# First attention by fours of heads: scores two pairs at a time, shifts and exps over two banks, value sums in twos

## The chip, the cores and the metric

The kernel runs on one core of one Trainium2 chip. Its time is the device time in microseconds (us) of one execution, and the median over several is given. A core has five engines, each with an in-order queue of its own: TensorE (PE) multiplies matrices into PSUM, VectorE (DVE), ScalarE (ACT) and GpSimd (POOL) work on SBUF, the first two on PSUM as well, and SyncE (SP) issues transfers. They are held together by semaphores: an instruction waits until a count is reached, and whatever stands behind it in its engine's queue waits with it.

## What is computed

Two layers over x of 4 x 2048 tokens of 256 values, each `x = x + attention(norm(x)) * silu(ffn(norm(x)))`. Only the attention of the first layer is changed. It has 16 heads of 16 values; a segment has 512 tokens, every eighth of which is a key (64 keys):

```python
q, k, v = (qkv[0] * scale, qkv[1], qkv[2])
q4 = q.reshape(B, H, S, SEG, hd)
k4 = k.reshape(B, H, S, SEG, hd)[:, :, :, ::DIL]
v4 = v.reshape(B, H, S, SEG, hd)[:, :, :, ::DIL]
scores = jnp.einsum('bhspd,bhskd->bhspk', q4, k4)
scores = scores.reshape(B, H, S, nb, BLOCK_M, Kn)
c = jnp.max(scores, axis=4, keepdims=True)   # over the 64 queries of a block, for each key
w = jnp.exp(scores - c)
den = jnp.sum(w, axis=-1) + 1e-10
num = jnp.einsum('bhsnmk,bhskd->bhsnmd', w, v4)
out = num / den[..., None]
```

The first layer's ffn is one product with a float8 weight and a bias. The second layer has attention with rotary positions over 2048 tokens and a mixture of eight experts.

## The kernel before

Four phases follow each other: `layers_phase` (the whole first layer, and the second layer's norm, projections and router logits), `attend_phase`, `experts_phase` and `combine_phase`. The change is in `layers_phase` alone. It walks over 16 segments m of 512 tokens; the second layer's projections belong to segment n = m - 1, so that two layers are in work at once. The order on each engine is written out by hand: PE's loop at L533, ACT's at L664, DVE's at L923.

Within a segment the heads go by pairs p = 0 to 7. Keys lie block-diagonally in `kbd`, so one product gives the scores of two heads: 128 partitions (2 heads x 64 keys) by 512 queries, which fills one PSUM bank. For a pair:

- `scores` (PE, L431): one product into the bank of the pair; pairs take the two banks of `sc` and the two of `tb` in turn, and a bank is free when the shift of the pair before last but one is done (L439)
- `shift` (DVE, L814): a maximum over each block of 64 queries (`keymax`, L819) and its subtraction (`shifted`, L821)
- the exp (ACT, L669) into one of NW = 3 buffers `wexp`
- `values` (PE, L443): the product with `vbd`, 64 columns wide, into one half of the single bank `ob`. It gives sums and denominators of two heads. Every even pair waits until the pair of halves before it has been copied (L449)
- `out_copy` (ACT, L585) copies `ob` into `oT` for every four heads; `turn` (PE, L453) turns it into `kv`, and `normalise` (DVE, L825) divides

PE's queue in a segment is: scores 0, 1, 2, values 0, scores 3, values 1, scores 4, values 2, turn 0, scores 5, values 3, scores 6, values 4, turn 1, scores 7, values 5, values 6, turn 2, values 7, `turn_second` (the normalised tokens of the second layer, for segment n, turned through `tb`), then `gate` 0 (L461, the first half of the ffn's product, into `pb`), turn 3, gate 1, and the projections of both layers, which end with the queries of segment m + 1.

On ACT each exp is followed, from pair 3 on every second time, by an `out_copy`; `part0` (L608, a cast of the rotated queries and keys of an older segment, 2048 wide) comes after the last exp, `second_turned` (L591, copies what `turn_second` wrote) after the last `out_copy`. On DVE the shifts stand with, between them, the second layer's normalised tokens (`second_norm`, L906, after shift 0), the end of the float8 rounding (`quantise_rest`, L796, after shift 1), `normalise` and the statistics of the next segment's tokens (`normed_tokens`, L896, after shift 5). POOL rotates halves of older queries and keys and computes inverse square roots (`inverse_root`, L309). SP stores and loads.

## Time and profile before

| what | us |
|---|---|
| median of 3 runs (lowest, highest) | 3757.64 (3751.62, 3771.84) |
| profiled execution, device time | 3755.5 |
| its span, first to last instruction | 3753.7 |
| PE busy | 3214.3 (86%) |
| DVE busy | 2698.2 (72%) |
| ACT busy | 2002.4 (53%) |
| POOL busy | 624.1 (17%) |

The profile is of one execution. "Busy" counts the time in which an engine works on at least one instruction; records of matmuls overlap, since they are pipelined. A product of 32-bit operands shows as two records. In the rows by stage (from:to in us of the span) the stages are: from segment 1's first gate product to segment 15's; from segment 0's first score product to its first gate product; the same for segment 8; from there to segment 9's first score product; and 5 us within segment 8. PEld is the load of PE's weights, the clock is the share of full speed granted to PE. In a row of the order of time, several records of the same kind stand together with their count; the bracket behind it is the time that the engine stood still ahead of it, and what ended that.

### The profile page before, as it was taken

To read this page: it belongs to the slowest core of one execution; us is meant where nothing else is said; L and a number is where in the kernel's file an instruction comes from. 1 tells how busy PE (TensorE), PEld (TensorE's weight loads), DVE (VectorE), ACT (ScalarE), POOL (GpSimd) and SP (SyncE) were. 2 spreads that over 40 slices of the span, in tenths; PEclk is the share of its full clock that TensorE was granted. 3 is DMA by queue.
4 is the path that set the end of the run, shared out by engine and by line. 5 is a ranking of instruction groups with operands and counts; after the bars stand their busy time and mean duration, and the time that the engine had idled before them with its cause. 6 is when DMAs were issued, how large, how long until landed. Compare 5 with 4: busy or idle time off the path is not lost. (4 is left out here: it accounts for less than half of the span.)

```text
span 3753.7 us, 67859 instructions
## 1 busy us (share of the span) xinstructions
PE 3214.3 (86%) x22678; PEld 1759.2 (47%) x22679; DVE 2698.2 (72%) x5118; ACT 2002.4 (53%) x3363; POOL 624.1 (17%) x954
## 2 busy tenths in 40 slices
PE   5888888884688988999899899999879899999976
PEld 3444444442233333333333333333358788888865
DVE  5677777775888877888888888888635556565557
ACT  2333433332177777888778788878842223232224
POOL 1122222221222221000000000000023233223310
PEclk9999999997599998999999999999989999999989
DMA  2122222223312222022222211220032111211149
GB/s 71 56 63 74 79 62 66 71 73 89 53 36 47 47 45 46 11 41 47 47 45 47 47 31 26 40 46 18 18 110 67 59 62 40 81 35 44 46 143 327
DMA packets 252770, 230.55 MB, mean 61 GB/s; under 512 B 60924, under 2 KB 235132, under 8 KB 252156
## 3 DMA queue, kind: packets, MB, share of 16 engines
q1 hardware_dynamic: 236040, 192.39, 20.1%
q0 software_dynamic: 16384, 33.64, 2.8%
q8 instruction: 205, 3.36, 0.4%
q14 instruction: 141, 1.16, 0.1%
HBM read 124.28 MB, written 101.06 MB: 60 GB/s over the span
## 5 line engine op out<-in xcount | busy, mean ns | idle before, releaser
L1488 ACT ACTIVATE at_ex<-at_so,keep_exp_scale 128x512 f32<-128x512 f32 (+1 forms) x2304 | 1348.8, 673 | 442.7 <-PE at_so L1382 239.1
L1515 DVE TENSOR_REDUCE at_best<-at_p 128x1 f32<-128x512 f32 (+3 forms) x2560 | 1393.2, 603 | 254.9 <-PE at_p L1364 164.6
L1364 PE MATMUL at_p<-at_ks,at_qs 48*128 48x512 f16 (+3 forms) x2560 | 805.5, 367 | 166.8 <-DVE at_best L1515 122.4
L1382 PE MATMUL at_so<-at_qs,at_ks 50*128 50x512 f16 (+3 forms) x2560 | 688.5, 358 | 19.0 <-issue 9.9
L1436 PE MATMUL at_ob<-at_ex,at_vs 128*32 128x512 f32 (+3 forms) x5120 | 605.4, 565 | 0.3 <-issue 0.2
L1786 ACT ACTIVATE e_hh<-e_hb,e_b1now 128x512 fp32r<-128x512 f32 x256 | 174.6, 689 | 591.6 <-PE e_hb L1721 514.8
L1364 PEld LDWEIGHTS at_p<-at_ks,at_qs 48*128 48x128 f16 x2560 | 216.6, 94 | 461.4 <-DVE at_best L1515 391.7
L1671 POOL DMA_INDIRECT e_xg<-s_xn,e_token x128 | 142.6, 1114 | 1682.7 <-DVE e_token L1816 1518.3
L1382 PEld LDWEIGHTS at_so<-at_qs,at_ks 50*128 50x128 f16 x2560 | 199.3, 95 | 459.6 <-ACT at_ex L1488 341.6
L1751 PE MATMUL e_ob<-e_w2h,e_hh 128*128 128x256 f32 x1024 | 296.0, 289 | 18.1 <-DVE e_og L1854 15.1
L1752 PE MATMUL e_ob<-e_w2l,e_hh 128*128 128x256 f32 x1024 | 291.8, 285 | 0.0
L1753 PE MATMUL e_ob<-e_w2h,e_hl 128*128 128x256 f32 x1024 | 291.6, 285 | 0.0
L1837 DVE TENSOR_SCALAR e_h<-e_hb,e_b1now 128x512 f32<-128x512 f32 x256 | 191.0, 746 | 116.3 <-ACT e_hh L1786 95.2
L451 PE MATMUL a_ob<-a_wexp,a_vbd 128*64 128x512 f32 x256 | 151.2, 675 | 116.2 <-ACT a_oT L589 91.2
L1719 PE MATMUL e_hb<-e_xh,e_w1h 128*128 128x512 f32 x512 | 210.4, 411 | 43.0 <-DVE e_h L1837 25.4
L1854 DVE TENSOR_TENSOR e_og<-e_ob,e_b2now 128x256 f32<-128x256 f32 x128 | 53.6, 423 | 239.2 <-PE e_ob L1753 202.9
L669 ACT ACTIVATE a_wexp<-a_shifted 128x512 f32<-128x512 f32 x128 | 80.6, 630 | 258.4 <-DVE a_shifted L821 258.4
L1721 PE MATMUL e_hb<-e_xh,e_w1l 128*128 128x512 f32 x512 | 206.8, 404 | 4.3 <-issue 4.3
L1347 PE MATMUL at_p<-at_identb,at_key_mask 64*128 64x64 bf16 x2048 | 208.9, 194 | 0.0
L1751 PEld LDWEIGHTS e_ob<-e_w2h,e_hh 128*128 128x128 f32 x1024 | 198.3, 194 | 21.3 <-DVE e_og L1854 16.5
L1720 PE MATMUL e_hb<-e_xl,e_w1h 128*128 128x512 f32 x512 | 207.5, 405 | 0.0
L1752 PEld LDWEIGHTS e_ob<-e_w2l,e_hh 128*128 128x128 f32 x1024 | 198.7, 194 | 0.0
(213 smaller groups left out, 4548.2 us busy)
## 6 DMA issues: line engine op xcount, KB each, us to landing
s_v<-a_v SPq DMA_DIRECT2D x64, 256.0 KB, 3.0
s_qk<-a_part SPq DMA_DIRECT2D x128, 128.0 KB, 2.4
at_vs<-s_v SPq DMA_DIRECT2D x32, 512.0 KB
s_eo<-at_empty SPq DMA_DIRECT2D x16, 1024.0 KB
e_w<-w SPq DMA_DIRECT2D x16, 1024.0 KB
f_rows<-s_eo SPq DMA_DIRECT2D x32, 512.0 KB, 8.3
at_qs<-s_qk SPq DMA_DIRECT2D x96, 128.0 KB
at_ks<-s_qk SPq DMA_DIRECT2D x96, 128.0 KB
```

The costliest lines, as they stand in the source:

```text
L1347: return pe.matmul(out[:, half * HALF:(half + 1) * HALF], mask[rows, half, :], identb[rows, rows], start=False, stop=last)
L1364: last = pe.matmul(out, qs[rows, buf, p, qt * P:(qt + 1) * P], ks[rows, buf, p, ch * SEG:ch * SEG + w], start=True, stop=ch != qc)
L1382: last = pe.matmul(so[:, v % NST, at:at + w], ks[rows, r, p, kt * P:(kt + 1) * P], qs[rows, r, p, q0:q0 + w], start=True, stop=not diag)
L1436: last = pe.matmul(ob[h * HW:(h + 1) * HW, SEG - w:SEG], vs[:, r, kt, h * HW:(h + 1) * HW], ex[:, (G * s + h) % NE, at:at + w], start=(kt ...
L1488: ev.done(act.activation(ex[:, v % NE, 0:width], so[:, v % NST, 0:width], ACT.Exp, scale=keep["exp_scale"][:, 0:1]), "ex")
L1515: ev.done(dve.tensor_reduce(best[:, row:row + 1, ch], p1[:, (at + e) % NP1, 0:wide(item)], AX, ALU.max), "mx")
L1719: pe.matmul(out, ah, bh, start=(j == 0), stop=False)
L1720: pe.matmul(out, ah, bl, start=False, stop=False)
L1721: last = pe.matmul(out, al, bh, start=False, stop=(j == len(pairs) - 1))
L1751: pe.matmul(out, high, w2h[:, u, m, :], start=(m == 0), stop=False)
L1752: pe.matmul(out, high, w2l[:, u, m, :], start=False, stop=False)
L1753: last = pe.matmul(out, low, w2h[:, u, m, :], start=False, stop=(m == HC - 1))
```

## The change

Heads go by fours ("doubles", d = 0 to 3, two pairs each). Both pairs' scores are written one behind the other into two adjacent banks, `sc` for even d and `pb` for odd ones (`tb` is no longer used for scores). Maxima, subtraction and exp each cover both banks in one instruction. Both pairs' value products go out one behind the other, into the two halves of `ob`. The order on PE becomes: scores 0, 1, 2, values 0, `turn_second`, scores 3, values 1, turn 0, values 2, turn 1, values 3, turn 2, gate 0, turn 3, gate 1. On ACT every exp from the second on is followed by the copy of the double before; `second_turned` goes behind the second exp's copy and `part0` ahead of the last copy. On DVE the order is shift 0, the second layer's tokens, shift 1, the rest of the rounding, shift 2, normalise 0, shift 3, normalise 1, the next segment's statistics, normalise 2. `gate` waits for the fourth shift, since `pb` holds scores until then.

```diff
@@ -148,7 +148,6 @@
         bqk1 = sb("bqk1", [P, 4])
         wvg1 = sb("wvg1", [P, DC, D + E])
         bv1 = sb("bv1", [P, D])
-        NW = 3
         x = sb("x", [P, 2, TT, D])
         stats = sb("stats", [P, 2, TT, 6])
         mv = sb("mv", [P, 2, TT, 2])
@@ -167,9 +166,9 @@
         qT = sb("qT", [P, DC, SEG])
         kbd = sb("kbd", [P, DC, H // DC, KN])
         vbd = sb("vbd", [P, H // 2, 2 * HW])
-        keymax = sb("keymax", [P, 2, NBLK])
-        shifted = sb("shifted", [P, 2, SEG])
-        wexp = sb("wexp", [P, NW, SEG])
+        keymax = sb("keymax", [P, 2, 2 * NBLK])
+        shifted = sb("shifted", [P, 2, 2, SEG])
+        wexp = sb("wexp", [P, 2, 2, SEG])
         oT = sb("oT", [P, 2, SEG])
         den = sb("den", [P, TT, G])
         rden = sb("rden", [P, TT, G])
@@ -205,13 +204,13 @@
         ob = ps("ob", [P, SEG])
 
 
-        def bank(p):
-            return sc[:, p % 4, :] if p % 4 < 2 else tb[:, p % 4 - 2, :]
-
-        NP0 = H // 2
+        def banks(d):
+            return sc if d % 2 == 0 else pb
+
+        NP0, ND0 = H // 2, H // 4
         counts = dict(
             var=1, rstd=1, xn=1, tr=1, trc=2, q=2, qc=2, kv=1, kvc=1, ff=2, ffc=2, quant=1, clip=1, round=2, wide=3,
-            s=NP0, shift=NP0, wexp=NP0, pv=NP0, oc=4, ot=4, norm=4, ytr=1, ytc=2,
+            s=NP0, shift=ND0, wexp=ND0, pv=NP0, oc=4, ot=4, norm=4, ytr=1, ytc=2,
             so=2, sog=2, ez=2, gate=1, x1=1, x1_out=1,
             var1=1, rstd1=1, xn1=1, xn1_out=1, tr1=1, tr1c=2, pj=4, pjc=4, rot=1, rot1=1, p1=1, p2=1,
             qk_out=4 * PART, vj=4, vjc=4, lc=4, v_out=NG, l_out=1)
@@ -428,27 +427,32 @@
                                          start=(k == 0), stop=(k == DC - 1))
                     ev.done(last, "q")
 
-                def scores(m, p):
-
-                    if p == 0:
+                def scores(m, d):
+
+                    f = d // (ND0 // DC)
+                    if d == 0:
                         ev.wait(pe, "kvc", m, 1)
                         ev.wait(pe, "sog", m, 0)
-                    f, a = p // (NP0 // DC), 2 * (p % (NP0 // DC))
-                    if a == 0:
-                        ev.wait(pe, "qc", m, f + 1)
-                    ev.wait(pe, "shift", m, max(p - 3, 0))
-                    ev.done(pe.matmul(bank(p), kbd[:, f, a:a + 2, :].rearrange("p a k -> p (a k)"),
-                                      qT[:, f, :], start=True, stop=True), "s")
-
-                def values(m, p):
-                    ev.wait(pe, "wexp", m, p + 1)
-                    if p == 0 and m >= 2:
+                        ev.wait(pe, "qc", m, 1)
+                    if d == 1:
+                        ev.wait(pe, "qc", m, 2)
+                    if d >= 2:
+                        ev.wait(pe, "shift", m, d - 1)
+                    for i in range(2):
+                        a = 2 * ((2 * d + i) % (NP0 // DC))
+                        ev.done(pe.matmul(banks(d)[:, i, :], kbd[:, f, a:a + 2, :].rearrange("p a k -> p (a k)"),
+                                          qT[:, f, :], start=True, stop=True), "s")
+
+                def values(m, d):
+                    ev.wait(pe, "wexp", m, d + 1)
+                    if d == 0 and m >= 2:
                         ev.wait(pe, "vjc", m - 2, TT)
                         ev.wait(pe, "lc", m - 2, TT)
-                    if p % 2 == 0:
-                        ev.wait(pe, "oc", m, p // 2)
-                    r = (p % 2) * 2 * HW
-                    ev.done(pe.matmul(ob[r:r + 2 * HW, :], vbd[:, p, :], wexp[:, p % NW, :], start=True, stop=True), "pv")
+                    ev.wait(pe, "oc", m, d)
+                    for i in range(2):
+                        r = i * 2 * HW
+                        ev.done(pe.matmul(ob[r:r + 2 * HW, :], vbd[:, 2 * d + i, :], wexp[:, d % 2, i, :],
+                                          start=True, stop=True), "pv")
 
                 def turn(m, g):
 
@@ -461,7 +465,7 @@
                 def gate(m, f):
 
                     ev.wait(pe, "quant", m, 1)
-                    ev.wait(pe, "qc", m, f + 1)
+                    ev.wait(pe, "shift", m, ND0)
                     for t in (2 * f, 2 * f + 1):
                         i = 0
                         for w in wf_piece:
@@ -532,17 +536,18 @@
                     queries(0, f)
                 for m in range(NSEG):
                     n, more = m - 1, m + 1 < NSEG
-                    for p in range(NP0):
-                        scores(m, p)
-                        if p >= 2:
-                            values(m, p - 2)
-                        if p >= 4 and p % 2 == 0:
-                            turn(m, (p - 4) // 2)
-                    values(m, NP0 - 2)
-                    turn(m, 2)
-                    values(m, NP0 - 1)
+                    for d in range(3):
+                        scores(m, d)
+                    values(m, 0)
                     if n >= 0:
                         turn_second(n)
+                    scores(m, 3)
+                    values(m, 1)
+                    turn(m, 0)
+                    values(m, 2)
+                    turn(m, 1)
+                    values(m, 3)
+                    turn(m, 2)
                     gate(m, 0)
                     turn(m, 3)
                     gate(m, 1)
@@ -663,17 +668,17 @@
                 widened(0, 1)
                 for m in range(NSEG):
                     n, more = m - 1, m + 1 < NSEG
-                    for p in range(NP0):
-                        ev.wait(act, "shift", m, p + 1)
-                        ev.wait(act, "pv", m, max(p - NW + 1, 0))
-                        ev.done(act.activation(wexp[:, p % NW, :], shifted[:, p % 2, :], ACT.Exp, scale=SCALE), "wexp")
-                        if p >= 3 and p % 2 == 1:
-                            out_copy(m, (p - 3) // 2)
-                        if p == 7 and n >= 1:
-                            part0(n - 1)
+                    for d in range(ND0):
+                        ev.wait(act, "shift", m, d + 1)
+                        ev.wait(act, "pv", m, max(2 * (d - 1), 0))
+                        ev.done(act.activation(wexp[:, d % 2], shifted[:, d % 2], ACT.Exp, scale=SCALE), "wexp")
+                        if d >= 1:
+                            out_copy(m, d - 1)
+                        if d == 1 and n >= 0:
+                            second_turned(n)
+                    if n >= 1:
+                        part0(n - 1)
                     out_copy(m, 3)
-                    if n >= 0:
-                        second_turned(n)
                     half_tanh(m, 0)
                     half_tanh(m, 1)
                     projected(n, 0)
@@ -811,16 +816,16 @@
                     st.then(dve.tensor_copy(vbd[0:KN, :, 0:HD], heads[0:KN, :, 0, :]))
                     st.mark(dve.tensor_copy(vbd[KN:P, :, HW:HW + HD], heads[KN:P, :, 1, :]), "kvc", m)
 
-                def shift(st, m, p):
-
-                    ev.wait(dve, "s", m, p + 1)
-                    ev.wait(dve, "wexp", m, max(p - 1, 0))
-                    blocks = bank(p).rearrange("p (n q) -> p n q", q=BLK)
-                    st.then(dve.tensor_reduce(keymax[:, p % 2, :], blocks, AX, ALU.max))
+                def shift(st, m, d):
+
+                    ev.wait(dve, "s", m, 2 * d + 2)
+                    ev.wait(dve, "wexp", m, max(d - 1, 0))
+                    blocks = banks(d)[:].rearrange("p i (n q) -> p (i n) q", q=BLK)
+                    st.then(dve.tensor_reduce(keymax[:, d % 2, :], blocks, AX, ALU.max))
                     st.settle()
                     st.mark(dve.tensor_tensor(
-                        shifted[:, p % 2, :].rearrange("p (n q) -> p n q", q=BLK), blocks,
-                        keymax[:, p % 2, :].unsqueeze(2).to_broadcast([P, NBLK, BLK]), ALU.subtract), "shift", m)
+                        shifted[:, d % 2].rearrange("p i (n q) -> p (i n) q", q=BLK), blocks,
+                        keymax[:, d % 2, :].unsqueeze(2).to_broadcast([P, 2 * NBLK, BLK]), ALU.subtract), "shift", m)
 
                 def normalise(st, m, g):
 
@@ -922,16 +927,17 @@
                 block_diagonal(st, 0)
                 for m in range(NSEG):
                     n, more = m - 1, m + 1 < NSEG
-                    for p in range(NP0):
-                        shift(st, m, p)
-                        if p == 0 and n >= 0:
-                            second_norm(st, n, 1)
-                        if p == 1:
-                            quantise_rest(st, m)
-                        if p >= 5 and p % 2 == 1:
-                            normalise(st, m, (p - 5) // 2)
-                        if p == 5 and more:
-                            normed_tokens(st, m + 1, 0)
+                    shift(st, m, 0)
+                    if n >= 0:
+                        second_norm(st, n, 1)
+                    shift(st, m, 1)
+                    quantise_rest(st, m)
+                    shift(st, m, 2)
+                    normalise(st, m, 0)
+                    shift(st, m, 3)
+                    normalise(st, m, 1)
+                    if more:
+                        normed_tokens(st, m + 1, 0)
                     normalise(st, m, 2)
                     gated(st, m, 0)
                     normalise(st, m, 3)
```

## Rows read from the trace of the kernel before

**Rows 1.** The page, its span and PE's busy time with records.

```profile
span 3753.7 us, 67859 instructions
PE 3214.3 (86%) x22678; PEld 1759.2 (47%) x22679; DVE 2698.2 (72%) x5118; ACT 2002.4 (53%) x3363; POOL 624.1 (17%) x954
```

**Rows 2.** By stage: us, busy PE, PEld, DVE, ACT, POOL, clock, DMA share, GB/s.

```profile
118.50:855.86 737.36, 633.79 (x2355) 333.44 (x2352) 535.56 (x1122) 289.53 (x476) 179.59 (x366) 0.95 0.24 69
47.74:70.97 23.23, 17.53 (x45) 5.17 (x44) 16.89 (x38) 8.03 (x13) 2.36 (x12) 1.00 0.00 0
511.34:538.74 27.40, 20.17 (x53) 6.67 (x52) 19.95 (x45) 9.80 (x15) 9.37 (x15) 0.94 0.22 63
538.74:563.09 24.35, 24.35 (x118) 16.83 (x116) 18.60 (x37) 10.86 (x20) 3.63 (x12) 1.00 0.28 82
523.00:528.00 5.00, 5.00 (x10) 1.59 (x10) 1.24 (x2) 0.63 (x1) 3.20 (x2) 0.66 0.01 3
```

**Rows 3.** Order of time on PE, segment 8: start, us, what, idle before.

```profile
511.34 1.88 PE L440 MATMUL a_sc<-a_qT,a_kbd 128*128 128x512 f32 x4
...
522.97 1.04 PE L451 MATMUL a_ob<-a_wexp,a_vbd 128*64 128x512 f32 x2 [2.96 <-ACT a_oT L589]
524.77 1.92 PE L440 MATMUL a_sc<-a_qT,a_kbd 128*128 128x512 f32 x2
...
535.25 1.04 PE L451 MATMUL a_ob<-a_wexp,a_vbd 128*64 128x512 f32 x2 [2.32 <-ACT a_oT L589]
536.22 0.66 PE L458 MATMUL a_kv<-a_ident,a_oT 128*128 128x128 f32 x4
536.81 1.07 PE L451 MATMUL a_ob<-a_wexp,a_vbd 128*64 128x512 f32 x2
537.81 1.09 PE L398 MATMUL a_tb<-a_ident,a_xn 128*128 128x128 f32 x8
538.74 1.47 PE L469 MATMUL a_pb<-a_wf_piece,a_xq 128*128 128x256 bf16 x12
```

**Rows 4.** Order of time on DVE, segment 8.

```profile
513.14 0.68 DVE L819 TENSOR_REDUCE a_keymax<-a_sc 128x8 f32<-128x512 f32 x1
...
514.47 1.37 DVE L778 TENSOR_SCALAR a_xn<-a_x,a_mv,a_rstd 128x256 f32<-128x256 f32 x4
...
517.08 0.69 DVE L799 TENSOR_SCALAR a_is_big<-a_square 128x1024 uint32<-128x1024 f32 x1
...
518.94 0.68 DVE L819 TENSOR_REDUCE a_keymax<-a_tb 128x8 f32<-128x512 f32 x1
...
526.72 0.69 DVE L819 TENSOR_REDUCE a_keymax<-a_sc 128x8 f32<-128x512 f32 x1 [3.72 <-PE a_sc L440]
...
528.06 0.17 DVE L829 TENSOR_SCALAR a_den<-a_kv 128x16 f32<-128x16 f32 x1
...
528.88 1.40 DVE L762 BATCH_NORM_STATS2 a_stats<-a_x 128x6 f32<-128x256 f32 x4
...
531.22 0.69 DVE L819 TENSOR_REDUCE a_keymax<-a_tb 128x8 f32<-128x512 f32 x1
```

**Rows 5.** Order of time on ACT, segment 8.

```profile
521.71 0.63 ACT L669 ACTIVATE a_wexp<-a_shifted 128x512 f32<-128x512 f32 x1 [0.69 <-DVE a_shifted L821]
522.25 0.58 ACT L589 ACTIVATE a_oT<-a_ob 128x512 f32<-128x512 f32 x1
```

**Rows 6.** Instructions of one line each, 1024 elements wide: ns least/median/most.

```profile
L1093 DVE TENSOR_REDUCE r_loc<-r_place x1: 1220/1220/1220, 957.9 to 957.9; 128x128 f32<-128x1024 f32 x1
...
L2029 DVE SCALAR_TENSOR_TENSOR f_th<-f_th,f_sc x16: 1221/1222/1222, 3644.2 to 3747.8; 128x1024 f32<-128x1024 f32 x16
...
L1978 ACT ACTIVATE f_th<-f_z x16: 1039/1041/1052, 3641.1 to 3741.8; 128x1024 f32<-128x1024 f32 x16
```

**Rows 7.** Order of time on PE, segment 8: the keys' value product.

```profile
504.05 1.15 PE L416 MATMUL a_kv<-a_wqkv,a_xnT 128*64 128x256 f32 x8
```

**Rows 8.** Order of time on POOL, segment 8: the end of the inverse root.

```profile
534.46 0.20 POOL L322 TENSOR_TENSOR a_rstd<-a_rstd,a_newton 128x4 f32<-128x4 f32 x1
```

## The prediction

> **What bounds the kernel now.** I read the page first: 3753.7 us of span, TensorE (PE) busy for 86% of it [rows 1]. That average says nothing about the changed stretch, so I went to the busy times by stage. The change lies in the first phase alone, 16 passes over a segment of 512 tokens. One pass repeats in two parts [rows 2]. From the first score product to the first gate product (the *front*) it takes 27.40 us in segment 8, and PE is busy for 20.17 of them. From there to the next segment's first score (the *back*) it takes 24.35 us, and PE is busy for all of them. The back is bound by PE and its instructions are not edited. So a microsecond gained in the front is a microsecond gained, as long as no other engine becomes late in the back. Passes 2 to 15 differ only in the front: 737.36 us for 14 repetitions less 14 x 24.35 leave a mean front of 28.3 us. The front of segment 0, which has no second layer beside it, is 23.23 us [rows 2].
>
> Next I read the front's order of time. VectorE (DVE) can subtract a pair's maxima every 1.33 us [rows 4], PE makes a pair's scores in 0.9 (two pairs, four records, in 1.88) [rows 3]. Neither keeps its pace: PE stands still 2.96 us before the values of pair 2, and 2.32 before those of pair 6, each time until ScalarE (ACT) has copied the one output bank [rows 3]. That copy is queued on ACT behind an exp that DVE has to feed first [rows 5], and behind the waiting product on PE stand the next scores, so DVE then waits 3.72 us for pair 5 [rows 4]. The front is bound by this circle of three in-order queues, not by any one engine. After the long stop PE also runs part of its work at its lower level, 1.2 GHz: the granted clock is 0.66 in the 5 us from 523, and one score product takes 1.92 us where two took 1.88 [rows 2, 3].
>
> **The change part by part.** Scores, values and shifts go by fours of heads (a "double", 4 per segment). The scores of two pairs go out together, up to three doubles ahead of the values, and no longer behind a value product that waits for its bank's copy. That takes the circle apart. The front is then a single chain on DVE, which I lay out from the first score product:
> - Both score products of double 0 must be done before DVE starts: 1.88 us [rows 3]. Before, DVE began at 1.80 anyway (513.14 against 511.34), since it was busy till then. Cost 0.1.
> - A shift over two banks. The trace of before has no such reduce out of PSUM. A reduce of 1024 elements takes 1.220 us, and an operation on 1024 elements that reads two PSUM banks 1.222, against 0.69 for 512 [rows 4, 6]. So a double costs 1.33 + 2 x (1.22 - 0.69) = 2.39 us instead of 2.66. From below: no less than this, as both rows agree to 2 ns; from above: 2.66, if two banks cost twice one. I take 2.39, the nearer row by size and by source.
> - In order on DVE: shift 0, the second layer's normalised tokens (2.61 with one shift from 514.47, so 1.28), shift 1, the rest of the quantising (1.86), shift 2, the first normalise (0.82), shift 3 [rows 4]. That is 1.88 + 2.39 + 1.28 + 2.39 + 1.86 + 2.39 + 0.82 + 2.47 = 15.48 us (the last shift counts to its end, 0.08 more). I checked what could interrupt it. Score double 1 is done at 3.6, needed at 5.6. Double 2 waits for shift 0 (4.35) and is done near 6.3, needed at 9.8. Double 3 waits for shift 1 (8.0) and is done near 10, needed at 13.1. The first turned heads come near 11.5, needed at 12.2.
> - Then what follows shift 3, each hand-over as the rows show it: 0.03 to ACT, an exp over two banks 1.04 (the activation on 1024 elements took 1.041) [rows 6], 0.49 until the copy of output double 2 that is queued behind it ends, 0.14 until PE starts [rows 3, 5], the last value pair 0.97 and the turning 0.59 [rows 3]. Sum: 15.48 + 3.26 = 18.7 us from first score to first gate product.
> - That needs a pair of value products to cost no more than one. Each fills 64 columns of the array; no row shows two of 512 elements side by side. The nearest is the keys' value product on the same 64 columns: 8 records of 256 elements, two halves, took 1.15 us [rows 7], where PE's rate in the scores (some 0.43 us for a record of 512 [rows 3]) asks 1.7 for them one behind the other. So two halves ran together, and I take the pair at 1.0. The other end is 1.9, two in a row.
> - The Trainium skill ("TensorE: Matmul & The Clock Gate", Part 3: Packing small matmuls) says that a weight load overlaps running products only when the row group differs. The two value products share all rows, so by that rule they would not overlap; rows 7 speak against it. It is the second rival below, whose price is worked out there from rows.
> - turn_second goes ahead of score double 3. It costs PE 0.93 us [rows 3], between value double 0 (done near 7.3) and score double 3, which waits for shift 1 at 8.0 anyway. Its copies on ACT (1.1 us) lie between the copy of output double 0 and the third exp, where ACT would wait for DVE. Free. If the tokens' turning came late, score double 3 still has 3 us before DVE needs it.
> - Queries for the second half of the heads must now be copied before score double 1, not pair 4. In the profile the copy is done when the first scores start, and the double goes into the bank that it frees. Free; the bound above is one copy, 0.6 us.
> - part0 (1.9 us on ACT) moves behind the last exp and stands ahead of the copy of output double 3. That copy ends near 19.5, and the third turning behind the first gate products wants it at 20.0. Nearly free; at worst 0.5 us, of which nothing is in my sum.
> - The gate products now wait for shift 3, since pb holds scores. It is done 3 us before. Free. SyncE's queue and the loads are not edited; the segment's stores keep their order.
> - Clock. PE now stops 2.5 us before value double 2 and 1.6 before double 3 (from this schedule). Stops of 2.96 and 2.32 us brought the lower level in some passes. In segment 8 the 5 us at 0.66 are 3.4 us at half rate, up to 1.7 us lost [rows 2]. Ends: 0 if PE stays at 2.4 GHz, 2.9 us if last values, turning and first gate products (1.56 + 1.31) all run at half rate. I take 1.2 per segment, since part of the slow work lies in the shadow of DVE.
>
> Sum at the upper clock level: 15 x (28.3 - 18.7) = 144 us, and segment 0, whose chain lacks the 1.28 us of the second layer, 23.2 - 17.4 = 6. Together 150. Less 16 x 1.2 = 19 for the clock: 131 us. The profiled execution took 3755.5 us (span 3753.7), the median of the runs shown is 3757.6. So 3755.5 - 131 = 3624.5, and with those 2 us of difference 3627.
>
> What is late next in the back? DVE and ACT enter it with the same work in the same order. POOL is the one whose slack shrinks: it starts the next segment's inverse root when DVE has written its input and needs 3.4 us (531.3 to 534.7 [rows 4, 8]). In the new order that input comes at 18.8 (DVE: shift 3, second normalise, 2.34 us of statistics), so the roots are there at 22.2. DVE asks for them after the second gated, near 22.7. It holds by half a microsecond.
>
> **The rivals.**
> - *Forecast*: DVE's chain of 15.5 us bounds the front. 3605 to 3645 with the clock's ends. Chance 0.70.
> - *Values in twos do not overlap.* The change then doesn't do what it says there. The last pair costs 0.9 more on the chain, and value doubles 0 and 1 push the first turning to 13.0, when DVE wants it at 12.2: 0.7 more. 16 x 1.6 = 26 us, so 3653. For it: single value products take as long on 64 columns as scores on 128 [rows 3]. Against: rows 7. Chance 0.12.
> - *The back gives some of it back*: POOL's root or part0 comes late by 1 to 2 us per segment and DVE, no longer PE, sets the back. In the back PE never stops now while DVE is busy 18.60 of 24.35 us [rows 2], so the first 2 us or so are absorbed; to cost 1 to 2 us a segment, the lateness must be 3 or more. 3643 to 3660. Chance 0.12.
> - *Slower.* The stops drop the clock and it stays down into the back. There all 24.35 us are PE's work; at half rate t us of it cost t more. From 9.4 us of back work at 1.2 GHz per segment the change is a loss; half of the back at the lower level (12.2 us more) gives 3627 + 195 = 3822. Against: the back is at 1.00 now after stops that were longer [rows 2]. Chance 0.03.
> - *Nothing to be seen*, by causes that cancel: chance 0.03.
>
> **How the numbers follow.** 3627 is the forecast's. The low end, 3602, is the clock at no cost (19 us) and a few us between runs; the high end, 3660, takes in no overlap and most of a partly returned gain. A measurement of this kernel can tell about 0.5%, 19 us, from no change. Faster by more: 0.70 + 0.12 + 0.12 + 0.01 = 0.95; within it 0.02; slower 0.03.
>
> **What would show it.** In the changed trace: reduce and subtract at 1.22 us each and exps at 1.04 (2.39 per double); value pairs as one group of four records in about 1.07 us (1.9 if the second rival holds); the first gate product 18.7 to 21 us after the first score, and no wait of DVE for scores from the second double on; PE stopping for ACT's copy before value doubles 2 and 3; the back still 24.35 us with PE busy throughout. I am wrong if DVE stands still before its shifts as it does now, if the back is longer than 25 us, or if the granted clock of the front falls below 0.85.

## The result, and the profile after

The changed kernel takes 3623.8 us (median of 4 runs, 3622.7 to 3629.0) against 3760.2 of the kernel before beside it: ratio 0.9638, 95% interval 0.9610 to 0.9666. The prediction was 3627, within 3602 to 3660, and faster. The profiled span fell from 3753.7 to 3620.9, by 132.8 us, where 131 were predicted.

PE does the same number of records. It stands still 54 us less and is busy 78.5 us less; 69.8 of the 78.5 lie in the value products (busy for 151.2 us before and 81.5 after), which now run two side by side. From the page of the changed kernel, the two lines that answer to [rows 1]:

```profile
span 3620.9 us, 67507 instructions
PE 3135.8 (87%) x22678; PEld 1743.3 (48%) x22679; DVE 2683.7 (74%) x4990; ACT 1989.6 (55%) x3299; POOL 624.6 (17%) x954
```

By stage, with the columns of [rows 2]: the first phase from segment 0's first score product to segment 15's first gate product (808.1 us before, 855.86 less 47.74 in [rows 2]), the front of segment 8, and its back.

```profile
46.43:721.05 674.62, 602.96 (x2533) 342.87 (x2532) 568.73 (x1102) 298.56 (x451) 188.13 (x402) 0.96 0.25 77
391.89:410.67 18.78, 15.46 (x54) 6.08 (x53) 16.84 (x26) 9.06 (x12) 7.02 (x3) 0.91 0.27 85
410.67:436.29 25.62, 24.53 (x118) 16.80 (x116) 20.80 (x49) 10.69 (x20) 6.00 (x24) 1.00 0.27 83
```

So the phase went from 808.1 to 674.6 us: 133.5 us, all of the gain. The rest of the kernel took 0.7 us more. Summed over segments, the fronts went from 448.4 to 302.1 us (-146.3) and the backs from 359.7 to 372.6 (+12.9). The front is 18.78 us in most segments (predicted 18.7; two are 20.09). The back, whose instructions nobody edited, is 25.62 in segment 8 and in most others, and no longer 24.35.

The order of time on PE through segment 8's front and into its back (start, us, what, idle before and its end):

```profile
391.89 1.88 PE L443 MATMUL a_sc<-a_qT,a_kbd 128*128 128x512 f32 x4
...
396.35 1.98 PE L443 MATMUL a_sc<-a_qT,a_kbd 128*128 128x512 f32 x4 [0.86 <-DVE a_shifted L826]
398.26 1.08 PE L454 MATMUL a_ob<-a_wexp,a_vbd 128*64 128x512 f32 x4
...
402.01 1.08 PE L454 MATMUL a_ob<-a_wexp,a_vbd 128*64 128x512 f32 x4
403.02 0.66 PE L462 MATMUL a_kv<-a_ident,a_oT 128*128 128x128 f32 x4
405.95 1.97 PE L454 MATMUL a_ob<-a_wexp,a_vbd 128*64 128x512 f32 x4 [2.27 <-ACT a_oT L594]
407.85 1.12 PE L462 MATMUL a_kv<-a_ident,a_oT 128*128 128x128 f32 x4
409.16 1.08 PE L454 MATMUL a_ob<-a_wexp,a_vbd 128*64 128x512 f32 x4 [0.20 <-ACT a_oT L594]
...
410.67 1.47 PE L473 MATMUL a_pb<-a_wf_piece,a_xq 128*128 128x256 bf16 x12
413.23 0.63 PE L462 MATMUL a_kv<-a_ident,a_oT 128*128 128x128 f32 x4 [1.09 <-DVE a_y L841]
```

And on DVE over the same stretch:

```profile
393.81 1.22 DVE L824 TENSOR_REDUCE a_keymax<-a_sc 128x16 f32<-128x1024 f32 x1
395.07 1.22 DVE L826 TENSOR_TENSOR a_shifted<-a_sc,a_keymax 128x1024 f32<-128x1024 f32 x1
396.21 1.37 DVE L783 TENSOR_SCALAR a_xn<-a_x,a_mv,a_rstd 128x256 f32<-128x256 f32 x4
...
406.22 1.22 DVE L826 TENSOR_TENSOR a_shifted<-a_pb,a_keymax 128x1024 f32<-128x1024 f32 x1
409.00 0.17 DVE L834 TENSOR_SCALAR a_den<-a_kv 128x16 f32<-128x16 f32 x1 [1.56 <-PE a_kv L462]
...
409.84 1.40 DVE L767 BATCH_NORM_STATS2 a_stats<-a_x 128x6 f32<-128x256 f32 x4
...
412.66 0.42 DVE L841 TENSOR_TENSOR a_y<-a_kv,a_rden 128x256 f32<-128x256 f32 x1
```

The order of time on ACT, same stretch:

```profile
404.26 1.06 ACT L674 ACTIVATE a_wexp<-a_shifted 128x1024 f32<-128x1024 f32 x1 [1.74 <-DVE a_shifted L826]
405.22 0.58 ACT L594 ACTIVATE a_oT<-a_ob 128x512 f32<-128x512 f32 x1
...
407.48 1.06 ACT L674 ACTIVATE a_wexp<-a_shifted 128x1024 f32<-128x1024 f32 x1 [1.68 <-DVE a_shifted L826]
```

And the changed kernel's exps of the whole phase, by their line (count, ns least/median/most):

```profile
L674 ACT ACTIVATE a_wexp<-a_shifted x64: 1056/1057/1061, 50.9 to 717.9; 128x1024 f32<-128x1024 f32 x64
```

What the reader is to see. Shifts stand one behind the other on DVE with no wait for scores: reduce and subtraction take 1.22 us each over two banks, an exp 1.057. A pair of value products is four records in 1.08 us, where one pair's product alone took two records and 1.04 to 1.07 before [rows 3]. Then PE stops for 2.27 us (405.95), the value double behind the stop takes 1.97 instead of 1.08 and the turning behind that 1.12 instead of 0.66: half rate. That slow work lies in the shadow of DVE's chain, so the front hardly grows. But DVE waits 1.56 us for that turning (409.00), and its normalise and the statistics behind it (409.84) are late. The normalise of output double 2 therefore ends near 413.1, and `turn` 3, which is already in the back (the prediction calls it the third turning), waits 1.09 us for it (413.23). With the clock kept up DVE waits only 0.21 us at this place (e_filler below), so 1.35 of the 1.56 us come from the half rate. The clock's price is paid in the back.

### The profile page after: what moved, and what is told of

Same layout as the page of the kernel before. It is cut to its first block and busy times, and to the rows that moved or that the text cites. A ratio compares the mean times of both kernels' runs of the same rounds, so it can differ in the third digit from the quotient of the medians.

```text
span 3620.9 us, 67507 instructions
## 1 busy us (share of the span) xinstructions
PE 3135.8 (87%) x22678; PEld 1743.3 (48%) x22679; DVE 2683.7 (74%) x4990; ACT 1989.6 (55%) x3299; POOL 624.6 (17%) x954
## 5 line engine op out<-in xcount | busy, mean ns | idle before, releaser
L1388 PE MATMUL at_so<-at_qs,at_ks 50*128 50x512 f16 (+3 forms) x2560 | 691.9, 361 | 18.7 <-issue 9.2
L1757 PEld LDWEIGHTS e_ob<-e_w2h,e_hh 128*128 128x128 f32 x1024 | 199.1, 194 | 22.9 <-DVE e_og L1860 16.5
L1759 PEld LDWEIGHTS e_ob<-e_w2h,e_hl 128*128 128x128 f32 x1024 | 199.1, 194 | 0.0
L1442 PEld LDWEIGHTS at_ob<-at_ex,at_vs 128*32 128x32 f32 x5120 | 117.9, 112 | 156.9 <-issue 106.9
```

The costliest lines, as they stand in the source:

```text
L1388: last = pe.matmul(so[:, v % NST, at:at + w], ks[rows, r, p, kt * P:(kt + 1) * P], qs[rows, r, p, q0:q0 + w], start=True, stop=not diag)
L1442: last = pe.matmul(ob[h * HW:(h + 1) * HW, SEG - w:SEG], vs[:, r, kt, h * HW:(h + 1) * HW], ex[:, (G * s + h) % NE, at:at + w], start=(kt ...
L1757: pe.matmul(out, high, w2h[:, u, m, :], start=(m == 0), stop=False)
L1759: last = pe.matmul(out, low, w2h[:, u, m, :], start=False, stop=(m == HC - 1))
```

## The experiments

Fronts and backs are summed over the segments of the trace, 16 fronts and 15 backs. Runs stand on three chips, on which the kernel before took about 3750, 3670 and 3767 us. The difference lies outside the first phase: what follows it takes 2890 to 2913 us in the traces of the first and third chip and 2800 to 2814 in those of the second. The phase itself repeats: 674.6, 675.3 and 675.6 us for the changed kernel in three traces. None of the three is from the chip of 3670 us, so that the phase takes the same there is argued from instruction times that agree, not shown. Times are compared as ratios to the kernel before beside them, and stages by the phase's sum. Ratios of different chips can't be compared to a few tenths of a percent: e_turn_late, 0.8 us slower in the phase than the changed kernel, has the better ratio (0.9615 against 0.9643). Where an expectation gives theories letters, A is what the author held at that time and the others are rivals, spelled out beside it.

**The changed kernel, as the base of the first group (e_changed).** No edit.

> The changed kernel once more, as the yardstick for the three beside it. Both theories: 3624 us, the front (first score product to first gate product) 18.8 us in segment 8, the back 24.4 to 25.7.

3617.0 against 3749.8: 0.9643 (0.9619 to 0.9667). Fronts 300.7, backs 374.6, phase 675.3: the same split again.

**The new order alone, without any doubling (e_order).** The kernel before, with PE sending each score product ahead of the value product three pairs older instead of two.

```diff
-                    for p in range(NP0):
+                    for p in range(3):
                         scores(m, p)
-                        if p >= 2:
-                            values(m, p - 2)
-                        if p >= 4 and p % 2 == 0:
-                            turn(m, (p - 4) // 2)
-                    values(m, NP0 - 2)
-                    turn(m, 2)
-                    values(m, NP0 - 1)
+                    for p in range(3, NP0 + 3):
+                        if p < NP0:
+                            scores(m, p)
+                        values(m, p - 3)
...
```

> The kernel before, with its pairs and its one-bank instructions, but every score product one pair earlier in TensorE's queue. Theory A (the gain is that no score stands behind a value product that waits for its bank's copy): VectorE's chain of 16.9 us of shifts and what lies between follows 1.8 us, then 0.7 for the exp, 0.6 to the copy's end and the value products, 3.5 for the last two value products, turnings and turn_second: a front near 23.5 us instead of 28.3, so 75 us less, near 3685, with VectorE waiting for scores under 0.5 us in each segment. Theory B (the gain is that there are fewer and wider instructions and paired values): no change, 3760.

3692.6 against 3749.8: 0.9838 (0.9814 to 0.9862). The fronts sum to 391.4 us (most of them 24.0 to 25.5), the backs to 359.7 as before. PE in segment 7:

```profile
391.74 1.94 PE L451 MATMUL a_ob<-a_wexp,a_vbd 128*64 128x512 f32 x2 [2.96 <-ACT a_oT L590]
...
402.08 1.04 PE L451 MATMUL a_ob<-a_wexp,a_vbd 128*64 128x512 f32 x2 [1.63 <-ACT a_oT L590]
```

On DVE in the same segment:

```profile
394.76 0.17 DVE L830 TENSOR_SCALAR a_den<-a_kv 128x16 f32<-128x16 f32 x1 [1.67 <-PE a_kv L458]
...
400.10 0.69 DVE L822 TENSOR_TENSOR a_shifted<-a_tb,a_keymax 128x512 f32<-128x512 f32 x1
```

So 57 of the 133 us come from taking the scores out from behind a waiting value product. Theory A had expected 75: the copies still stop PE for 2.96 and 1.63 us, and one product runs at half rate, 1.94 us. DVE no longer waits for scores behind them, but it waits for the turned heads (1.67 us here, 0.3 to 1.7 over the segments), which the expectation had at nothing. The remaining 76 us come from the other edits of the change; the part on the prediction says which.

**Value sums not side by side (e_serial).** Each product of a pair becomes 128 columns wide with zeros in the other pair's half, the second added on the first, so that the two must follow each other. The result is the same.

```diff
-        vbd = sb("vbd", [P, H // 2, 2 * HW])
+        vbd_wide = sb("vbd", [P, H // 4, 12 * HW])
+        vbd = vbd_wide[:].rearrange("p d (i x) -> p (d i) x", i=2)[:, :, 0:2 * HW]
...
-                        ev.done(pe.matmul(ob[r:r + 2 * HW, :], vbd[:, 2 * d + i, :], wexp[:, d % 2, i, :],
-                                          start=True, stop=True), "pv")
+                        ev.done(pe.matmul(ob[:], vbd_wide[:, d, i * 4 * HW:(i + 1) * 4 * HW], wexp[:, d % 2, i, :],
+                                          start=(i == 0), stop=(i == 1)), "pv")
```

> The changed kernel, with each value product widened to 128 columns (the other pair's columns are zero weights and are added in), so that the two of a double must run one behind the other. Theory A: each pair of value products takes 1.9 us instead of 1.1; 0.86 more on the chain at the last double and up to 0.7 at the first turning, 1.6 in each of 16 segments: 26 us more than the changed kernel, near 3650. Theory B, that TensorE's work does not matter here since it stops 2.3 us in each front anyway: within 5 us of the changed kernel.

3626.8 against 3749.8: 0.9669 (0.9643 to 0.9695). The order of time on PE in segment 8:

```profile
410.90 1.96 PE L454 MATMUL a_ob<-a_wexp,a_vbd 128*128 128x512 f32 x4 [1.15 <-ACT a_oT L594]
412.69 0.60 PE L462 MATMUL a_kv<-a_ident,a_oT 128*128 128x128 f32 x4
```

Its front and back by stage:

```profile
396.85:417.05 20.20, 16.67 (x54) 8.04 (x52) 18.38 (x34) 9.61 (x13) 7.33 (x5) 1.00 0.25 79
417.05:441.40 24.35, 24.35 (x119) 16.81 (x117) 19.45 (x40) 10.14 (x19) 5.69 (x23) 1.00 0.29 87
```

A double in a row takes 1.88 to 1.96 us against 1.08. The pair in twos does run side by side, and the rival of the prediction that it doesn't is refuted. In the changed kernel's records the second product of a double starts 0.01 us after the first (398.26 and 398.27). The front grows by 1.42, near the 1.6 of that rival. But the kernel loses only 7 us in the phase (682.6), not 26, because the back fell to 24.35. Longer value products leave PE a stop of 1.15 us instead of 2.27, the turning behind it takes 0.60 instead of 1.12, and the granted clock is 1.00 in both stages. That was the first sign that the back's 1.27 us belong to the stop.

**Maxima and subtractions one bank at a time (e_one_bank).**

```diff
-                    st.then(dve.tensor_reduce(keymax[:, d % 2, :], blocks, AX, ALU.max))
...
+                    for i in range(2):
+                        half = blocks[:, i * NBLK:(i + 1) * NBLK, :]
+                        top = keymax[:, d % 2, i * NBLK:(i + 1) * NBLK]
+                        st.then(dve.tensor_reduce(top, half, AX, ALU.max))
...
```

> The changed kernel, with maximum and subtraction over one bank each, two of each per double. Theory A (VectorE's chain bounds the front): 0.27 us more per double, four on the chain, 17 us more than the changed kernel, near 3641, and a front of 19.9. Theory B (the gain comes mostly from the wider instructions): a large part of the 136 us goes, 3680 or more.

3627.8 against 3749.8: 0.9683 (0.9649 to 0.9718). Fronts 319.5 (+18.8 against 300.7, or 1.18 us each, where 4 x (2.66 - 2.39) = 1.08 is the pure saving), but backs 366.3 (-8.3): in 8 of the 14 full ones the back is 24.35 again. Net 10.5 us, where theory A had 17. Again the slower front got something back from the clock.

**Keep PE going through its stop (e_filler).** 16 transposes of the identity into a free bank, behind turn 0, where PE waits.

```diff
                     turn(m, 0)
+                    if n >= 0:
+                        ev.wait(pe, "tr1c", n, 2)
+                    for t in range(16):
+                        pe.transpose(tb[:, 1, (t % TT) * P:(t % TT + 1) * P], ident[:], ident[:])
                     values(m, 2)
```

> The changed kernel, with 16 extra transposes of the identity on TensorE in the 2.27 us stop ahead of value double 2 (1.9 us of work at the upper clock level, into a bank that nobody reads then). Theory A (clock): they end before the copy that TensorE waits for, the following products run at 2.4 GHz, front 18.8, back 24.35 in all segments: 17 us less than the changed kernel. Theory B (the back is late for another reason, or extra work in a stop costs): back unchanged at 25.6, no gain or some us more.

3511.6 against 3669.8: 0.9581 (0.9559 to 0.9602). The order of time on PE in segment 8:

```profile
395.43 1.91 PE L550 MATMUL a_tb<-a_ident 128*128 128x128 f32 x16
397.86 1.08 PE L454 MATMUL a_ob<-a_wexp,a_vbd 128*64 128x512 f32 x4 [0.52 <-ACT a_oT L598]
```

The back of that segment by stage:

```profile
402.58:426.93 24.35, 24.35 (x119) 16.82 (x117) 19.60 (x42) 10.72 (x20) 5.99 (x24) 1.00 0.29 87
```

Useless work in the stop makes the kernel faster. All full backs are 24.35 and all fronts from segment 1 on 18.77; the phase is 658.8 us, 16.5 less than e_changed. The value double behind the filler takes 1.08, at the upper level. This shows the cause of the back's growth, since nothing but PE's idle time was changed.

**Copies of the output ahead of the exps (e_copy_first).** ACT copies output doubles 1 and 2 before exps 2 and 3, which wait for DVE.

```diff
                     for d in range(ND0):
+                        if d >= 2:
+                            out_copy(m, d - 1)
                         ev.wait(act, "shift", m, d + 1)
...
-                        if d >= 1:
-                            out_copy(m, d - 1)
+                        if d == 1:
+                            out_copy(m, 0)
```

> The changed kernel, with ScalarE's copies of output doubles 1 and 2 ahead of the exps of doubles 2 and 3 instead of behind them. Theory A (VectorE's chain, then the hand-overs behind the last shift; 1.28 us per segment lost in the back because the product pair after a 2.27 us stop runs at 1.2 GHz and the next normalise comes late): the copy leaves the path, front 18.3 instead of 18.8; TensorE's stop shrinks to about 1.8 us, and if the clock stays up the back is 24.35 instead of 25.6: 25 us less than the changed kernel, 0.9575 of the kernel before. If the clock still falls, only 8 to 15 us less. Theory B (the back's 1.28 us come from GpSimd's late inverse root): front 18.3, back still 25.6: 8 us less.

3508.2 against 3669.8: 0.9561 (0.9541 to 0.9582). The order of time on PE in segment 8:

```profile
394.51 1.08 PE L454 MATMUL a_ob<-a_wexp,a_vbd 128*64 128x512 f32 x4 [1.69 <-ACT a_wexp L676]
...
397.73 1.08 PE L454 MATMUL a_ob<-a_wexp,a_vbd 128*64 128x512 f32 x4 [1.55 <-ACT a_wexp L676]
```

On ACT in the same segment:

```profile
393.40 1.06 ACT L676 ACTIVATE a_wexp<-a_shifted 128x1024 f32<-128x1024 f32 x1 [0.49 <-DVE a_shifted L828]
...
398.33 1.91 ACT L617 ACTIVATE a_part<-a_rot 128x2048 f16<-128x2048 f32 x1 [0.66 <-POOL a_rot L338]
```

Front 18.19 us, backs 24.65, phase 652.7: 22.6 less than e_changed. PE now stops 1.69 and 1.55 us, and for the exp itself, no longer for the copy behind it; both value doubles take 1.08. The copy's 0.58 is off the end of the chain, and the clock stays up without filler (granted 1.00 over the whole phase, against 0.96 in the changed kernel). The back is 0.3 us longer than the 24.35 that theory A expected with the clock up: ACT's `part0` waits for POOL's rotation (0.66 in the row above), and the last output copy, which `turn` 3 wants, stands behind it. e_best tests that.

**The second layer's turning back to its old place (e_turn_late).** `turn_second` and its copies go behind the last value double, ahead of the gate.

```diff
                     values(m, 0)
-                    if n >= 0:
-                        turn_second(n)
                     scores(m, 3)
...
                     turn(m, 2)
+                    if n >= 0:
+                        turn_second(n)
                     gate(m, 0)
```

> The changed kernel, with turn_second back behind turn 2 and its copies back behind the last output copy. Theory A: its 0.93 us of TensorE lie on the chain again, front 19.7, 14 us more than the changed kernel; stops get longer, so the back stays at 25.6. Theory B (moving it was free of effect, TensorE stops anyway): no change.

3526.8 against 3669.8: 0.9615 (0.9597 to 0.9634). PE in segment 8:

```profile
411.51 1.04 PE L397 MATMUL a_tb<-a_ident,a_xn 128*128 128x128 f32 x8
412.38 1.47 PE L473 MATMUL a_pb<-a_wf_piece,a_xq 128*128 128x256 bf16 x12
414.07 0.63 PE L462 MATMUL a_kv<-a_ident,a_oT 128*128 128x128 f32 x4 [0.22 <-DVE a_y L841]
```

The front is 19.64, longer by 0.87, which is the turning's own time. The back is 24.76, shorter by 0.87: `turn` 3 must wait for the late normalise in either order, here only 0.22 us after the gate. The phase is 676.1, +0.8 and not the 14 I had expected. Moving the turning was worth nothing *as long as the clock delays DVE*. With the clock kept up it is worth its 0.87: in segment 5 of this trace the double behind the stop took 1.08, and there the front is 19.64 and the back 24.35. It is one segment; no run with the clock kept up throughout was made.

**The statistics of the next tokens ahead of the last shift (e_stats_early).**

```diff
                     normalise(st, m, 0)
-                    shift(st, m, 3)
-                    normalise(st, m, 1)
                     if more:
                         normed_tokens(st, m + 1, 0)
+                    shift(st, m, 3)
+                    normalise(st, m, 1)
```

> The changed kernel, with the next segment's statistics (2.34 us of VectorE) back ahead of the last shift, where the kernel before has them ahead of its last two. Theory A (VectorE's chain up to the last shift bounds the front): front 21.1, and the back falls to 24.35, since nothing is left for the late turning to delay: 35 us more in the fronts, 17 less in the backs, 18 us more than the changed kernel. Theory B (the order on TensorE alone carries the gain): front 18.8 to 19.3, within 8 us of the changed kernel.

3612.2 against 3669.8: 0.9839 (0.9814 to 0.9864). Fronts of 24.56 us, not the 21.1 expected, and backs of 24.4 to 25.6 in most segments; phase 753.7, 78.4 more than e_changed where 18 were expected. The order of time on DVE in segment 7:

```profile
396.57 2.31 DVE L772 TENSOR_SCALAR a_veps<-a_mv 128x4 f32<-128x4 f32 x1
```

On POOL:

```profile
396.52 2.34 POOL L338 TENSOR_TENSOR a_rot<-a_rot,a_prod 128x1024 f32<-128x1024 f32 x1
```

On PE:

```profile
403.41 1.98 PE L454 MATMUL a_ob<-a_wexp,a_vbd 128*64 128x512 f32 x4 [6.03 <-ACT a_oT L594]
...
406.22 2.60 PE L473 MATMUL a_pb<-a_wf_piece,a_xq 128*128 128x256 bf16 x12
```

The chain on DVE was expected to grow by the statistics alone, 2.34 us. Two things came on top. A `tensor_scalar` of 128x4 took 2.31 us instead of 0.17: it ended with POOL's rotation, which had started 0.05 us before it. And after a stop of 6.03 us PE did the value double, the turning and the first gate products (2.60 instead of 1.47) at half rate. So this run prices more than the statistics' place alone: 2.34 us of the 5.8 that the front grew by are their own time.

**The changed kernel and the best version (e_changed2, e_best).** e_best is e_copy_first with the last output copy ahead of `part0` as well:

```diff
+                    out_copy(m, 3)
                     if n >= 1:
                         part0(n - 1)
-                    out_copy(m, 3)
```

> The changed kernel, as the yardstick on this chip: 0.964 of the kernel before; front 18.8, back 25.6 in most segments.

> The run with the output copies ahead of the exps, and the last output copy ahead of part0 as well. Theory A (what was left of 0.3 us in that run's back, 24.65 against 24.35, is the third turning, which waits for an output copy behind part0, which waits for GpSimd's rotation): front 18.2, back 24.35, 4 us less than that run and 27 less than the changed kernel, 0.957 of the kernel before. Theory B (the 0.3 us come from VectorE's normalise): back still 24.65.

3633.8 and 3607.1 against 3766.9: 0.9647 (0.9609 to 0.9685) and 0.9576 (0.9545 to 0.9608). The phase is 675.6 and 651.6 us, front 18.19 and back 24.56 in segment 8. By the phase's sum e_best is the fastest version found, 24 us below the changed kernel; its lead over e_copy_first is 1.1 us in the phase, and the two ratios' intervals overlap. Theory A had expected a back of 24.35 and 4 us, so the copy behind `part0` is only a third of what was left. The rest is theory B's: in e_best DVE's normalise of output double 2 ends at 400.74, and `turn` 3 starts at 400.88, 1.49 us into the back, where it started at 1.31 in e_filler.

**Everything but the shifts off DVE's chain, first try (e_chain).** e_best, with `quantise_rest` behind the last shift, the statistics behind the second gated, the next tokens later, and POOL's rotation released by the first shift.

```diff
-                        ev.wait(pool, "quant", n + 2, 1)
+                        ev.wait(pool, "shift", n + 2, 1)
...
                     shift(st, m, 1)
-                    quantise_rest(st, m)
                     shift(st, m, 2)
...
                     shift(st, m, 3)
+                    quantise_rest(st, m)
                     normalise(st, m, 1)
-                    if more:
-                        normed_tokens(st, m + 1, 0)
...
```

> The run before this, with two steps taken off VectorE's chain: the end of the rounding (1.86 us) goes behind the last shift, the next segment's statistics (2.34 us) behind the second gated, its normalised tokens behind rest; GpSimd's rotation starts after shift 0 instead of after the rounding. Theory A (the chain up to the last shift bounds the front, the back has 3.9 us of VectorE to spare): front 16.4 instead of 18.2, back 24.4 to 25.2, 15 to 27 us less. Theory B (VectorE as a whole is the next bound: 38.6 us of work in a pass of 42.5 with its waits in fixed places): front 16.4, back 26 or more, no gain.

3799.6 against 3766.9: 1.0098 (1.007 to 1.0126), slower than the kernel before. Neither theory's front of 16.4 came: most fronts are 25.4 or 27.4, most backs 29.3 or 30.4, and the phase is 843.9. The order of time on DVE in segment 7:

```profile
420.20 7.53 DVE L785 TENSOR_SCALAR a_xn<-a_x,a_mv,a_rstd 128x256 f32<-128x256 f32 x4
427.65 1.21 DVE L826 TENSOR_REDUCE a_keymax<-a_pb 128x16 f32<-128x1024 f32 x1
...
453.96 1.38 DVE L785 TENSOR_SCALAR a_xn<-a_x,a_mv,a_rstd 128x256 f32<-128x256 f32 x4 [2.96 <-POOL a_rstd L321]
```

On POOL:

```profile
420.46 2.36 POOL L335 TENSOR_TENSOR a_rot<-a_qk,a_rope 128x1024 f32<-128x1024 f32 x1 [10.54 <-DVE a_shifted L828]
422.78 2.38 POOL L336 TENSOR_TENSOR a_prod<-a_qk,a_rope 128x1024 f32<-128x1024 f32 x1
425.24 2.34 POOL L338 TENSOR_TENSOR a_rot<-a_rot,a_prod 128x1024 f32<-128x1024 f32 x1
...
448.93 2.12 POOL L317 TENSOR_TENSOR a_newton<-a_newton,a_veps 128x4 f32<-128x4 f32 x1
```

Four `tensor_scalar`s of 128x256, 1.37 us before and after the change, took 7.53. The first took 0.41, the other three 2.42 to 2.49 each, one beside each of POOL's three rotations (2.34 to 2.38). In the other direction a Newton step of POOL, 0.20 us where nothing meets it, took 2.12 beside DVE's `tensor_tensor` of 2048 elements with two inputs in SBUF (448.71 to 450.99), and DVE waited 2.96 us for the roots. The Trainium skill ("SBUF — State Buffer", Who interferes with whom) says that VectorE and GpSimd share one port pair as an exclusive lock for a whole instruction, that a `tensor_scalar` can take it, that VectorE with two SBUF inputs contends with GpSimd's reads, and that a reduce never contends. The tensor_scalars' 7.53 against 1.37 and POOL's 2.12 against 0.20 agree. For the reduce these runs show only the one out of PSUM, at 1.22 us beside POOL's rotation in the changed kernel.

**The same, with POOL kept apart (e_chain_apart).** The rotation now waits for the second layer's tokens, the statistics stand between the first gated and the last normalise, and half of the residual goes ahead of the next tokens.

```diff
-                        ev.wait(pool, "quant", n + 2, 1)
+                        ev.wait(pool, "xn1", n + 1, 1)
...
                     gated(st, m, 0)
+                    if more:
+                        normed_tokens(st, m + 1, 0)
                     normalise(st, m, 3)
                     gated(st, m, 1)
+                    residual(st, m, 0)
                     if more:
                         normed_tokens(st, m + 1, 1)
-                    residual(st, m, 0)
```

> The run with all copies ahead, again with the end of the rounding behind the last shift, but GpSimd's rotation now starts only when VectorE has finished the second layer's normalised tokens, and the statistics stand between the first gated and the last normalise, the next tokens behind residual's first half. Theory A (in the run before, GpSimd's rotation and VectorE's tensor_scalar on SBUF shut each other out: four of them took 7.5 us instead of 1.4; apart, the shorter chain pays): the four take 1.4 us, front 16.4, back 25.2, a pass of 41.6 instead of 42.75 us, 0.953 of the kernel before. Theory B (VectorE as a whole is the bound, and moving its work only moves the wait): front 16.4, back 26.4 or more, 0.957 or worse.

3534.3 against 3665.6: 0.9645 (0.963 to 0.966). The order of time on DVE in segment 8:

```profile
401.32 1.38 DVE L785 TENSOR_SCALAR a_xn<-a_x,a_mv,a_rstd 128x256 f32<-128x256 f32 x4
...
408.83 0.17 DVE L836 TENSOR_SCALAR a_den<-a_kv 128x16 f32<-128x16 f32 x1 [1.35 <-PE a_kv L462]
```

On PE:

```profile
414.98 1.09 PE L462 MATMUL a_kv<-a_ident,a_oT 128*128 128x128 f32 x4 [0.61 <-DVE a_y L843]
415.86 2.59 PE L473 MATMUL a_pb<-a_wf_piece,a_xq 128*128 128x256 bf16 x12
```

The tokens take 1.38 us again, which shows that POOL's place was the cause of the 7.53. The front is 18.44 to 18.85, not the 16.4 expected, and the back 25.43 to 26.55; the phase is 679.4, 28 us worse than e_best. With 1.86 us less ahead of it DVE is at the first normalise 10.5 us after the first score; the turned heads come at 11.8, as in the changed kernel, and it waits 1.35. At the end the turning waits for DVE's normalise (0.61), and the gate products run at half rate (2.59). The half rate comes in every third segment only, of which 8 is one; the others from 3 on have a front of 18.44 and a back of 25.43 with the gate products at 1.47. In these too DVE is late in the back: in segment 7 PE waits 0.54 us for it ahead of the turning of the gated values (377.05). The chain on DVE could not be shortened this way: with the quantising gone, the chain through PE's turning takes its place.

## Why the prediction was right, point by point

- *The circle of three queues bounds the front.* Right. e_order breaks it with no other edit and gains 57 us. Where the other 76 lie is read from rows. In e_order's segment 7 the last shift ends 20.7 us after the first score, in the changed kernel's segment 8 15.6. Of these 5.1 us the statistics are 2.3, which the changed kernel has behind its last shift, DVE's wait for the turned heads 1.7, and the two-bank shifts 1.1. What follows the last shift takes 4.8 us there and 3.2 here. Undone one at a time from the changed kernel, the statistics' place costs 78.4 us (e_stats_early), the two-bank shifts 10.5, the overlap 7.3 and the turning's move 0.8. The last three are smaller than their own front terms, since the clock gives something back, and the first is larger than its 35, since it meets POOL and a longer stop; so these prices don't add up to 76. What the fours are worth by themselves, with half as many hand-overs to ACT, wasn't run.
- *The chain on DVE and its size.* Right nearly term by term: shifts 1.22 + 1.22 with 2.39 as their step (401.75 to 404.14 for a whole double), exp 1.057 where 1.04 was taken, the first turning in time (11.8 where 11.5 was said and 12.2 needed). A wait of DVE for the second turned heads, 0.21 with the clock up, was not in the sum; it lies behind the last shift. From first score to first gate 18.78 against 18.7. With the clock kept up (e_filler) the fronts sum to 299.1, 149.3 less than before, where the sum at the upper level was 150.
- *The value pair.* Taken at 1.0 from the keys' product, 1.08 measured, 1.96 when made serial. The rival is refuted, and its price was misjudged too: its front term of 1.6 is about right (1.42 measured), but the longer products fill PE's stop, and the kernel would have lost 7 us and not 26. The sentence of the Trainium skill ("TensorE: Matmul & The Clock Gate", Part 3: Packing small matmuls) is on weight loads alone, which it lets overlap running products only when the row group differs. That products which share all rows don't overlap either was the prediction's own step from it, and it is not what these runs show: four records in 1.08 us, the second product starting 0.01 us after the first.
- *PE's stops.* Taken at 2.5 and 1.6, measured 2.27 and 0.20. With the clock kept up the second is 1.54 (e_filler), as taken; here it is short because PE comes out of the slow double 0.9 and the slow turning 0.5 us later.
- *The clock.* The size was about right and the place was wrong. Taken: 1.2 us a segment, 19 in all, as time of the front. Measured, the changed kernel's trace against e_filler's: 3.0 in the fronts, 12.9 in the backs, 15.9 in all. So the fronts gained 146.3 us where I had 131, and the backs lost 12.9 where I had nothing. The two errors cancel; that the total came out within 2 us is luck to that extent. The step that failed is the one by which the back absorbs the first 2 us of lateness on DVE. DVE waited 1.56 us for the turning at half rate, and the normalise behind it feeds `turn` 3. That is due 1.3 us into the back (e_filler) and started 2.6 us into it, ahead of nearly all of DVE's slack. The mark that I had set for being wrong, a back over 25 us, was met (25.62). The rival in which the back returns 1 to 2 us a segment happened, by another cause than its own, along with a front nearly free of the clock's loss. Two segments of the changed kernel confirm the path: in 1 and 9 the double behind the stop of 2.27 took 1.08, and there the back is 24.35. One reading was off: the lower level came not in some passes of the kernel before but in every one from segment 1 on, behind the stop of 2.96.
- *POOL's root.* Wanted ready by 22.2, asked for at 22.7. In the trace the statistics end at 412.3 and the root at 415.6, 23.7 us after the first score, later than said since the statistics waited for the turning; DVE's next tokens start at 415.87 without a wait, since DVE too is late. In e_filler, where it is not, the root is there at 22.4 and the tokens start at 22.7. The slack is 0.3 us in both, where half a microsecond was said.
- *The turning of the second layer and part0 at no cost.* Right: 0.8 us and 1.1 us in all by e_turn_late and e_best. For the first I had come to expect 14 before the run, wrongly: it would have needed a `turn` 3 that isn't late. What the move brings is 0.87 us a segment where the clock stays up (segment 5 of e_turn_late), and next to nothing where the back gives it away.
- *Segment 0.* Front 17.54 against 17.4. Its back is 1.2 us shorter than before (17.63 against 18.86), where the trace of before shows products at half rate; e_filler shows them there too and has 18.86. So the full backs lost 14.1 us and this one gave back 1.2. Why the clock fell there in two kernels and not in the third stays open.

## What to carry to other kernels

Where engines hand work round a circle of in-order queues, take the producer's next work out from behind the consumer's wait; read the gain from the chain that is left, instruction by instruction. A stop of TensorE (here of 2.27 us) can have a price that falls on the work behind it. Follow that work to whoever waits for it, even if it now lies in another engine's shadow. Shortening the stop (a copy ahead of an exp that waits anyway) brought 22.6 us here, twice what the two-bank shifts are worth. And before an instruction of VectorE on SBUF is moved, look at what GpSimd does at that time.

## What was not expected of the hardware

- VectorE and GpSimd shut each other out for whole instructions: 7.53 us for 1.37 (four `tensor_scalar`s beside three rotations), 2.31 for 0.17, and 2.12 for 0.20 the other way round.
- One stop of 2.27 us on PE was followed by about 1.3 us lost at half rate (1.97 + 1.12 for 1.08 + 0.66), while stops of 1.69 and 1.55 (e_copy_first) or 1.15 and 1.53 (e_serial) were followed by none from segment 1 on. 16 transposes of the identity in the stop, 1.91 us of them, kept it up. Nor does each stop of 2.27 bring the loss: in six segments of e_stats_early and in two of the changed kernel the same stop was followed by a value double of 1.08, and in nine of e_one_bank a stop of 2.59 was. What tells them apart stays open.
- As expected, and now shown for the reduce: an instruction of DVE that reads two PSUM banks costs no more than its elements ask, 1.22 for 1024 where 512 took 0.69 [rows 4]. ACT's exp over a double took 1.057 where 512 elements took 0.63 [rows 5]; it reads and writes SBUF, so it says nothing of PSUM.
